# Another written order of turns on five engines, and other PSUM banks, in a kernel of two transformer layers

## The reference

```
x = x + gla(norm(x)) + local(norm(x))
x = x + delta(norm(x)) + experts(norm(x))
```

## Time and profile before

| | us |
|---|---|
| median of 3 runs | 1379.96 (1379.38 to 1380.86) |
| span of the profiled execution, first to last instruction | 1391.4 |
| PE busy (matmuls) | 1265.5, 91% |
| PEld busy | 1007.5, 72% |
| DVE busy | 947.4, 68% |
| ACT busy | 738.6, 53% |
| POOL busy | 679.6, 49% |
| mean of DMA | 166 GB/s |

### The profile page before, as it was taken

The page is one execution under the profiler, slowest core; times in us unless marked ns, Lnnn a source line. Parts: engine busy times, 40 slices in busy tenths (PEclk is TensorE's granted clock), DMA queues, the critical chain, the costliest instruction groups (busy, mean ns, idle before and its releaser), DMA issues.

```text
span 1391.4 us, 43177 instructions
## 1 busy us (share of the span) xinstructions
PE 1265.5 (91%) x18034; PEld 1007.5 (72%) x18034; DVE 947.4 (68%) x2038; ACT 738.6 (53%) x2084; POOL 679.6 (49%) x677
## 2 busy tenths in 40 slices
PE   5776869999999999899999899989999999889898
PEld 3444557777678788678887688767787778778776
DVE  3667688966777876677688668775758775475434
ACT  5577857654745663446765366435774355133221
POOL 3545346763473556256565355443736545304422
PEclk8899899999999999899999999999999999999999
DMA  5101056744366367265676357635565644647662
GB/s 198 59 11 62 1 196 191 228 123 149 114 206 210 128 196 247 95 203 181 215 229 192 104 191 231 206 134 172 168 200 166 206 167 160 221 147 233 189 226 99
DMA packets 90721, 231.44 MB, mean 166 GB/s; under 512 B 9376, under 2 KB 15648, under 8 KB 90400
## 3 DMA queue, kind: packets, MB, share of 16 engines
q1 hardware_dynamic: 90384, 228.09, 50.9%
q10 hardware_dynamic: 144, 0.59, 0.1%
HBM read 225.50 MB, written 3.15 MB: 164 GB/s over the span
## 4 chain that ended last, share of the span: by engine, by line
PE 71%; DVE 12%; issue 4%; ACT 3%; DMA 2%; POOL 1%; DVEq 0%; SPq 0%; ACTq 0%
PE bank L968 15%; PE bank L921 15%; PE bank L831 8%; PE bank L958 4%; PE bank L939 4%; PE bank L616 4%; PE bank L949 2%; PE bank L932 2%; PE bank L687 2%; PE bank L675 2%; DVE ogate L1405 2%; PE bank L711 2%; PE bank L651 1%; PE bank L721 1%; PE bank L661 1%
## 5 line engine op out<-in xcount | busy, mean ns | idle before, releaser
L1802 POOL TENSOR_TENSOR vgate<-vgate,xT 128x512 f32<-128x512 f32 x256 | 323.5, 1288 | 137.8 <-DMA vgate<-gates 137.6
L921 PE MATMUL bank<-wv,vgate 128*128 128x128 f32 x2048 | 258.7, 281 | 5.4 <-POOL vgate L1802 4.7
L921 PEld LDWEIGHTS bank<-wv,vgate 128*128 128x128 f32 x2048 | 247.3, 195 | 16.1 <-issue 11.0
L968 PE MATMUL bank<-ogate,wo 128*128 128x256 f32 x1024 | 251.4, 390 | 3.9 <-DVE ogate L1405 2.7
L968 PEld LDWEIGHTS bank<-ogate,wo 128*128 128x128 f32 x1024 | 191.7, 194 | 35.4 <-issue 10.2
L1405 DVE TENSOR_TENSOR ogate<-ogate,bank 128x1024 f32<-128x1024 f32 x128 | 153.4, 1211 | 37.1 <-PE bank L958 35.6
L1746 POOL TENSOR_TENSOR rot<-rot 128x512 f32<-128x512 f32 x64 | 81.9, 1280 | 108.4 <-DVE rot L1071 108.4
L1516 ACT ACTIVATE prob<-prob,mx 128x128 f32<-128x128 f32 (+1 forms) x256 | 96.0, 377 | 55.9 <-DVE mx L1095 55.6
L1758 POOL TENSOR_TENSOR prob<-prob,rsum 128x256 f32<-128x256 f32 (+1 forms) x64 | 60.1, 939 | 113.9 <-DVE rsum L1098 113.9
L1695 ACT ACTIVATE mprob<-bank,mmin 128x256 f32<-128x256 f32 x128 | 59.3, 469 | 100.7 <-DVE mmin L1394 100.4
L616 PE MATMUL bank<-wqkv,hT 128*128 128x512 f32 x192 | 103.9, 640 | 5.4 <-ACT hT L1452 4.7
(11 more groups left out here) (236 smaller groups left out, 2574.9 us busy)
## 6 DMA issues: line engine op xcount, KB each, us to landing
vgate<-gates SPq DMA_DIRECT2D x128, 512.0 KB, 4.5
ogate<-gates SPq DMA_DIRECT2D x128, 512.0 KB, 4.2
wv<-in_wv_moe SPq DMA_DIRECT2D x128, 256.0 KB, 4.9
wo<-in_wo_moe SPq DMA_DIRECT2D x128, 256.0 KB, 4.7
kv<-values SPq DMA_DIRECT2D x128, 128.0 KB
local<-in_local SPq DMA_DIRECT2D x1, 1715.0 KB, 10.5
wqkv<-in_wqkv SPq DMA_DIRECT2D x2, 768.0 KB, 7.0
x<-in_x SPq DMA_DIRECT2D x8, 128.0 KB, 8.5
```

Of the source, the lines that this page charges most:

```text
L921: i = nc.tensor.matmul(out[:, n * D:(n + 1) * D], xg[:, e, n * P:(n + 1) * P], m.wv[slot][:, e, :], start=(q, n, e) == (0, 0, 0), stop=(q, ...
L968: i = nc.tensor.matmul(out[:, 0:T], m.wo[slot][:, e, :], cg[:, e, :], start=(h, q, e) == (0, 0, 0), stop=(h, q, e) == (MH - 1, 1, EQ - 1))
L1802: i = tt(gate[:, e:e + half, :], gate[:, e:e + half, :], spread(m.xT[b % 2][:, :], 1, half), ALU.mult)
```

## The change

All six strings are replaced by others of the same length in letters (each letter stands as often as before, in another sequence), and one wait is added in DVE's `wo`. The new strings were drawn with a price on changes of the array's form and on stretches of low activity of TensorE. The steps, their instructions, the streams, tiles and transfers stay as they are.

```diff
 TENSOR_TURNS = (
-    "aaaaaaaaabbabaXGGGGbabbbaaabaabGaaabbbbbGcaabcbGbbbccbbGcGaabbabGaacaaacGGGbaGcbacbbcaaabbbGaabbGaaabbabbGbcab"
+    "GaaaaGGGaaaaabbaXbabbabaaabbGbaabbaaabbGcabGacbbcbcbbGcbbGabbaabGcaaGGGcGaaabbcacbaGcbbbbaaGabbbbaaGaaabbbGGac"
 ...
 VECTOR_TURNS = (
-    "VaaaaaaaaabaabbbaabGGaaGGaabGGGbaaGbGGaaGbGGcbbGGbcbcGGbbccccbGaaaaGcaacGaacbGGGbbcccGGcbbGGbaaGGaabGGabaGGGaa"
+    "VaaaaaaaGaabaaabbGGbGabGGGaabbGaabGGGaaGGaabcGGGcbbcGbbbcccbcbGaaaaGcGaacGcbaaGGbbGGbGGcccGGcbGGbbaaGbGaaGGGGa"
 ...
 SCALAR_TURNS = (
-    "aaaaaaaaaaaabaaababXGGaGGaGbabbaaaaaaabbbaabbababacabbcbbcbcbabbGaGbbaabGaaaacaaacGGGaaacGabcbbabaaabbaaaababb"
+    "GaaaGaaGGaaaaGaaabaaabbaaXababbaabbbaaaabbaaabaaacbacbbcbbcbbabbGabbGaabGaacaaGGGacaaGcbaaabcabababbbbaabbaaab"
 ...
 GPSIMD_TURNS = (
-    "aaaaaaababaaGabGaGabaGaGaGbbGGbbaaaGaaaaabGGbbGaaGaaGabaGaaGbGbbbaaaGababWaWWaabbGWGWaWaaGaGaWabWabWGaGWDbWWbG"
+    "aaaaaaaabaGbGGabaabaGGaaGaaGbGbbbaaaGaaaaabGGbGGGbabaGaaGGaaababbabaaGaaaababbWWabaaWaGWGWGWaGaaaWbbGGWGWDGWbbW"
 ...
 SYNC_TURNS = (
-    "xxxGGGGGGGGGGGGGGGGGGCGvvvoooGGGGvvvoovGvGvoGovGovvoovovvCvvvvooooooGvoGvGGGGGvvvvooEoGGvoxvooovoovCoovvvvooGG"
+    "xxxGGGGGGGGGGGGGGGGGGGGGGGCvvvooovvvooGGvGGovovovovvoovCvvvvovovoooooGvGGGGvvvvGGvoExoooGGoovvooovCvoovvvoovGG"
 ...
 BANK_TURNS = (
-    "01234567012346512734061527346152731523463175314753675143651741036574160351673452071360747236504372650243762453"
+    "76543210765204375643275062743502674023645036243562403256410325641025364105321067541305247057132045712345731425"
 ...
@@ -1101,6 +1101,10 @@
         bank = banks.of("wo", b, l)
         out = filled(bank)[:, 0:T]
         x = m.xmid[b % 2] if l else m.xn0T[b % 2]
+        before = earlier(b, l, 1)
+        if before:
+            read = banks.of("w2", *before)
+            v.wait_ge(read.emptied, read.use)
         tt(m.xloc[:, :], x[:, :], out, ALU.add).then_inc(bank.emptied, 1)
```

More of the change, by code:

```diff
@@ L88 @@
[L88 to L92, removed]
@@ new lines @@
+    "bacbabcbbacbbGaacabbazGGGabaCbbcCAGaFbaabbACbcbabaabcVbcbAVabcVcAAaacAPPGzFaacAVDbAAbGAPFVbPVAFcAAGCPaAcaaCVbb"
+    "bPbAVbDbAAVbPbADDbPDVDDACcDADDAaAVDVDDaAcGDaADAaVADcGVDaDDPADVAADDPADVaDDPbbPAGPbAaDFADDPAaaGPGGaGAVbbVbDVbbDD"
+    "VbADAbFADDFFDVbDDAGbADAVcADDcPcEaacaPPAPacaGAaaabPbAPaDAbVaVcbbbcDbzDbbAaPabbAAbDaCAPCDDPGaaAVacaCGVaDAAbaPAbD"
+    "DPcbaDGaDDFDDAcVcGVVDADAcbPPDDADbbDDVDGGGGDDbADzbADDAbFAPPbVbFVVDADDbFDVDDAVDAPDDVDAcCGGCFDDAPAEVVAPDAPDDcACAV"
+    "AVADPDDAcPDAAaVAaaaDDVPDcPDDAaaGGDDaacbbDAVVAPbaDADPDDaDDAaDGDDbbDbaDDaDaADDVVbPDbDDbADVDDbbaPDbAcVDcaaAacGAAa"
@@ new lines @@
+    "FPcDAbPcbaGaGAbbGGbaAAbVAPPbAbbAAVbAPbPbAEFAAVAPaVAFPAAVAcaPVDAaDDAADcAPDDGacDaAVDDbPbDaPDDbVDDAAcDAaDVDDaADVD"
+    "DcDPzDDADAGPDDADaVDDPaDbGDDaaDaDDVbDbbPaaabbaaACbbADAabCAcVacVPcVcACPcAAGFAGbPGVbPAVAAVAbGPzbbVAbbCPAAbEAbGVbb"
+    "APbGcAACcFAFGPacFVaaaDAVPcaaAPPaaaAcaAVaVVAaaaCPDVGDDaaAADVAPDDGaaDAaDDAAVAaPDaPDDAVDDAAVDAbDPDDbPDADDbGDADDAP"
+    "ADbVDDbPDADDbFDGbVDDbADAGPAbDDVDbGPbVbbbVcDAPAAEbcbAGGbVGcGbbVcbAbVcbbFGbaaacDFaaGFPaaacAAPAaGPcVaVcAVcAzDAPAV"
+    "DDCVDCADDPGAAPAbVGPPCGbDFADDGbADAVAVDDPVDDAVPDADAbbAbDPDDbPDDbADbDDFDADDAbbAPDbDDPcDADDVcDADDFAPcAcDFVVcAVzADD"
@@ new lines @@
+    "APAEVVCAVDCADDAVAPDVDDPCVPDAPDDAADVADDPDDAPDADAVADDPDFDDAVDAAPAPDDVPDVDDAFDADDAVADPDDPDADFDDAAFVAPPDDVAVAAVAPD"
+    "PADEAADVADPDADPAADVADDPDAPAADDAPDDAPDVDVDDVAADAPDDPADVDDVAADVADDPDPADDVAADVADDPDPADDVAADVAPPADAPPE")
+VECTOR_TURNS = (
+    "VaaaaaaaGaabaaabbGGbGabGGGaabbGaabGGGaaGGaabcGGGcbbcGbbbcccbcbGaaaaGcGaacGcbaaGGbbGGbGGcccGGcbGGbbaaGbGaaGGGGa"
+    "abaaabbcGcbacbbbaabcccaacGzGCaCabaabbCCCCCCCCbacbacFbbAcabaFAGaaFcccVVGGcGGFGcGOOaaAcGAzcCGCFVaabOOVbbAGFbGAGG"
+    "DDGVVGFGFOOcccFDGAcADCCbCCbbCVVCbCOOCDADDADVVDDcDOODDaaADAVVDDaacOcDADGVVDADaaDODADAVVODbbbOGbODaOaFAFAGFDGbFV"
+    "VDbGGbGDGOObDGAFDFAFGDVGDFVGDFDVVGDcccAGGcAGDDDcEaOacDaacOaOOabGaaabbGAGbGADaVVcccbcbbzDCDbCaaOODaaACCCACCCCCa"
+    "acDDVVaOOabDADbbADcbDcDDGFFFcccDVVGDFOObcDbDADDAVVDGDbGzDCOOGGGGCGbGAGGAFDVVFDDFDFVVDOODFDVVDADcADCCCDDDCOOECV"
+    "VDGGDCACACcaDcOOaDVVGADGAGGDGDGFOOADFaaADVVDFaaDFDDcccaaDcbaOOabbVVDbDADADDDDbDGDbaaDOOaaVVDbDDbDDDDADcAccaaOO"
+    "aVaGVFDDcccAbDAcbbGbbOOaaAbGAGGbGGOObVAVGGAGGEFOOAAaaVVFFOOFAcADVVDDDOODAcAcDDaDaGGGDbDGbbDaaaDbDVVDOOccDcADAD"
+    "DVDVcDzDCODCODGGDAGaDAGDbDbDaaDVVaabDbDaaDaOOaCCcCCcCcAVCACCVccccOOFAFAbVVGFbbGOOFAbVVGAzCbCbbOOEAbAVVcOacOacA"
+    "CCCFACFFaaDDCaaVGCDVFOOaacccGaacGAFCAGGGCaaDGaaDGGDVDVVVaOOaADGGADGDGDaaGDGOODAVVGGADDDDOODVAbDVADbbDDbDOODADb"
+    "ADbDDFDbVDVFOODGADbFDAFDVVGDbbbcbOEOcAbcAGVVbbGbGGGcccGGGcGGVVFaaGGaacFDDDFaaGGcOOaacAFGAGFVVGGcccDcOzOCDACVAV"
+    "DDDCCCCCCOOCCAVDVbADGbbDGbDDGFOOADFADVDVFFDDOODVADbAVDbbDDbDDOODFADADcDDcDOOcDFAADFcccVVFDcFDzVOODDDCAECVAVVDD"
+    "CCODCDCCCDCCODADVVADDDOODVVADDADDOODVVADADFDFOODAFDAVVDFDDOODVFADVADDDFDOODFDAFAFDDDVVOODVAVADEOODDADADDOODVVA"
+    "DDADOODADADDDVDVOOADDADVDVOODVVADADDOODVVADADDOODVADADOOE")
@@ new lines @@
+GPSIMD_TURNS = (
+    "aaaaaaabaGbGGabaabaGGaaGaaGbGbbbaaaGaaaaabGGbGGGbabaGaaGGaaababbabaaGaaaababbWWabaaWaGWGWGWaGaaaWbbGGWGWDGWbbW"
+    "WWaaWWaaDWDDWaDDWDDaWbGbDaaDWbDGWDGWbDDWDGDWGWGGDaaaaaaabaGbGWWbbaaaaWaaaWabbWGDWWDbDDDDDWDGGbGGDWDDWDWDWDDWWD"
+    "WGWWGWGGWaaWaaaaabaWbDDDWDDDDDDbaDaaDaWbDDWDDWWaaaGabbabaWGGbWGGWaaWDWWaaGWbGaabWDDDDWDDWDDDGDDGDWDbDaDaaaWbaa"
+    "aaWWWWbGWbWbWbWaWaaWaaaaaGDGWaGaaWaaGWWGaGaWaGWGWDDWDbDDbDDDDbDWDDDWDDbWGWbWbbWbGWGGWGaaGaaaGaaaGDGWWWWWWbGbWW"
+    "WDWDDDbDDbDDDDDDDDWDWWWDWWWWWWWDDDWDDWDDDWDDWDDWDDDWDWWWWWDDDWWDWDDDWDWDWDDDWDDD")
@@ L137 @@
+    "GGGoovvvvvovGGGGovEvoxoCvvoovvoovvoovvovovooGGGGGvoovooExvovovovoGGvoovvvoGGovovovoCovvovovvovoEGvGGGGxoovvooo"
+    "vvvCovGGvoGGvoovvooovovovovvoEGvGGGGvvGGGGooovvvovvoovooCvvovvooooovovvvoEvvvvovoCvoovoovovoovovvoovoovvvooEvo"
+    "ovoooovvvoovvvoovoooE")
 BANK_TURNS = (
-    "01234567012346512734061527346152731523463175314753675143651741036574160351673452071360747236504372650243762453"
-    "70247534704732750431250742051742051275213724516307475167552156035076435041367513756416341653413605145065141056"
@@ new lines @@
+    "14723156745612741536724153746125374615270324761052410671521527152604671501674502675107264107561047645762574254"
+    "72547562477745627354627546725436246572645732645763246573425746256257645246436345634564352065203654360456026050"
+    "26402460602462046256426270627021670221647216746727461264327164327412674371263746213472634746731243712642731274"
+    "16237416237162345136514231435271432714372172412713421432147324731624716241706241061024061420615062450416526041"
+    "20416504124652104561246514251456521451654162514625462504625460540642135206435120645306421021346214362431062743"
@@ new lines @@
+    "10264107246072146071240674260726072607246027462067407042704272407402452045250570457026470527502652672407265472"
+    "64576452767520456714062751407164053167453021675016257625071271560506527150267106761701572501750150751701253701"
+    "23710257130271320710321037103170317031270231723075321607532064532726450316403756403574603174631043760064736403"
+    "72640324360274302703647023670245023674530274630273465603267043206734023467023647032770437205243765240637125406"
+    "71457254307253401523401352704352740725403754304752034725014375021734506274316047136540716354071653461534167514"
@@ L152 @@
+    "63571647513467156")
 PACKS = {
```

42 lines of the change are left out of this document (8 added, 34 removed).

## The result

The changed kernel takes 1444.24 us (median of 4 runs, 1443.81 to 1449.11), the kernel before beside it 1380.41 us. The ratio is 1.0477, 95% interval [1.0427, 1.0528]: slower by 64 us, where 1369 was forecast. The forecast and its range (1350 to 1394) are wrong, and the sign with them.

The account below looks back on a forecast made before the run. It took TensorE's queue, busy 91% of the span, plus losses in it as the bound. Terms of -2 - 9 + 2 - 3 + 1 = -11 us on 1380 gave 1369 us, with 1350 to 1394 for 8 in 10.

Parts of the forecast that it names:

- SP's queue: Transfers now issued ahead of gsend(0) in the start should be through before the gates are ready: 0, at most +4 us.
- The middle stretch's idle time: Sign to check: TensorE's idle time in the 840 us after the first 210 stays within 5 us of 35.
- The start: First 210 us: two TensorE waits go as gv and fuse come earlier, -9 us, ends -15 and +5.
- Refills: TensorE's "issue" stops in bursts of small matmuls, read as late instruction refills: +2 us, ends -10 and +25.
- Clock: TensorE's half-speed time, 111 us before, shrinks with fewer very thin stretches: -3 us, ends -15 and +5.
- Forms: TensorE's changes of the array's form fall from 698 to 680: -2 us, ends 0 and -4.
- banks: A product may wait for another one's bank to be emptied: 0, ends -3 and +3 us.
- Hops: Delta chain between TensorE and DVE: less TensorE work between du and ds, +1 us, ends 0 and +11.
- The added wait: DVE's wait on its own product of the layer before, at least 5 turns earlier: taken as 0.
- both slower ones: Rivals: stops outweigh the start, 1398 us with six more, chance 0.19; delta hops bind and start gives nothing, 1391, 0.10.
- The first: Rival: stops in D's bursts behind the start outweigh its gain; slower from three more, 1398 us with six; chance 0.19.
- My last sentence: Sign: forecast wrong if idle time after 210 us moves more than the start; then stops or waits no count shows.

Follow-up runs that it names:

- the control: The kernel before with each of the six gate and weight slots loaded once and never again: 1356.01 us, ratio 0.9826.
- start_new: The changed kernel's turns of the first 150 us, then the rest in the order and banks of the kernel before, without the added wait: 1372.29 us, ratio 0.9948.
- shift: The kernel before with 32 extra matmuls of 8 columns in TensorE's gk turn at about 34 us: 1391.53 us, ratio 1.0064.

## Why the prediction was wrong, point by point

- **The step that failed** is the one with the heading "SP's queue": "So they should be through before the gates are ready: 0, and at most +4 us on the whole start if not." Nothing in the runs speaks against it for the start, but it was the only term in the sum for when expert gates arrive. Behind the start they stood at nothing, and no reason was given, though two orders with other distances between TensorE's last use of a slot and POOL's next turn for it were being compared. In its place the runs showed some 50 us of 64 that vanish with the expert loads (64 to 13). The middle stretch's idle time was to stay within 5 us of 35 and came to 83.9. The row that should have opened this term is the first of the waits of POOL above, 137.6 us in 41 waits, 74.5 of them between 210 and 1050 us; I had read only TensorE's waits and took POOL's for idle time of an engine that is not the bottleneck. Its size was not small: by the control, the kernel before itself pays 24 us (1380 - 1356, give or take 9) for its expert loads.
- **The start, -9:** right in size. By start_new it is -7.5 us, and TensorE did 8.7 us more in the first 210 us. The values are stored at 14.6 us (I had said before 25), TensorE's wait of 5.47 us is gone (its longest for the rotation before 60 us is 2.0), DVE's of 5.27 us for kv has become three that sum to 3.7, and the first value product stands 9 us earlier than in the earlier trace rows:

```profile
182.10 2.02 PE L921 MATMUL bank<-wv,vgate 128*128 128x128 f32 x16 [0.73 <-POOL vgate L1806]
```

  The spreading loads now begin at 20.7 us in place of 38.0.
- **Refills, +2:** the direction was right, the size too small, and within its ends: 26 stops with 39.1 us for 18 with 28.8, +10. I had put them down to the order of small matmuls alone. With small expert loads they are 27.5 us after and 15.4 before, without them 15.0 and 9.3: more than half of each goes with the expert loads, and some 5 of the 50 us that vanish with the loads are refills. The trace agrees with the Trainium skill ("Runtime: NRT & Kernel Launch", section "Instruction fetch mechanics") on blocks of 256 instructions. It agrees with its saying that fetching is mostly hidden only by count, since 144 packets make 26 stops at L831; these cost 39.1 us of 1448 all the same.
- **Clock, -3:** 0.954 x 1447.8 leaves 133 us at the lower level, against 111: 22 more, where the forecast had a gain. The windows above show it falling behind a gap (0.50 from 710 us on), so it is in part a result of the gaps; it costs at most half of 22 us.
- **Forms, -2, and banks, 0:** nothing in the runs isolates them; TensorE's busy time (1270.1 against 1265.5) leaves the forms a few us. The bank string did not only change its sequence: bank 1 is taken 126 times in place of 192, bank 7 166 times in place of 104. The kernels without expert loads keep their banks, so a cost of the banks that doesn't depend on the loads lies in what is left there.
- **Hops, +1 (0 to +11):** not isolated. What of them doesn't depend on the loads lies in the 20 us or so that are left without expert loads, of which refills are 5.7 (15.0 against 9.3).
- **The added wait, 0:** agrees, within 9 us.
- **The rivals:** both slower ones named other mechanisms than the one found, and their 1398 and 1391 were short by 46 us and more. The first named stops: there are 8 more of them, and they cost 10 us more, where it reckoned 31 for six. My last sentence did hold: "the forecast is wrong if idle time after 210 us moves by more than the start does". It moved by 60 us.

What stays open: which turns make the last 20 us; how the 50 us divide between POOL and DVE coming sooner for a load and loads that land late behind kv transfers; and how much would come back if only the distances, or only SP's order, were changed. No kernel here tried that. start_new, which takes the new start and the old rest, is the fastest kernel here that computes the whole result, 1372.3 us.

## What to carry to other kernels

When two orders of the same work are compared, take for each load the distance from its slot coming free to its next use, and hold it against the time from issue to landing, which is not one number: 5.3 us on the mean here, 4.0 even with a quarter of the bytes, and 11.4 behind a row of other transfers. A wait of an engine that is half idle is no loss only as long as nothing behind it in its queue, and nothing in the bottleneck's own next turns, needs it: read the waits of every engine for DMA before a term is set to 0. An order's parts can be cut at a time at which each engine's prefix is complete and joined to the rest of another order; that shows in two runs which part pays.

## What the runs showed of the hardware

- Small loads are hardly sooner there: 128 KB in 4.0 us where 512 KB took 5.3, on the mean, in the same traffic. What stands ahead counts for more: the 512 KB took 4.6 us with fewer than four kv transfers (128 KB each) issued in the 8 us before, and 11.4 us with four to eight.
- The refills of TensorE's instructions start later when data loads are there. With full, small and no expert loads, in the same order of instructions, the stops are 39.1, 27.5 and 15.0 us. A packet of instructions itself takes 1.1 us on the mean in all three. What changes is its start: from TensorE passing place 150 of a block to the start of the packet that belongs to it, it is 3.8, 3.1 and 2.3 us on the mean. When a packet starts, TensorE has at most some 300 places of its queue left to the one at which it would stop, and a burst of small matmuls can run through 256 in a few us: 68 of them, with their weight loads 136 places, took 1.06 us.
- A small matmul is no cheaper than its weight load. In shift the 64 extra ones stream 8 columns each, against weights of 128 columns, and took 0.18 us each, where 68 of the 32x32 form took 1.06 us together. The clock was 0.63 over these 12 us, which explains less than a factor of two. The timeline of TensorE, and the window over it, in which the weight loads (PEld) are busy 11.88 of 12 us:

```profile
32.61 11.51 PE L744 MATMUL bank<-gla 16*128 16x8 f32 x64
```

```profile
32.00:44.00 12.00, 12.00 (x72) 11.88 (x70) 0.00 (x0) 0.92 (x2) 0.00 (x0) 0.63 0.00 0
```
